# A four-layer image network on one core: halves of neighbouring images interleaved, GpSimd's adds moved to VectorE, and the offsets stage written out as a pipeline

## The chip, the core and the metric

The kernel runs on one core of a Trainium2 chip. The metric is the device time of one execution in microseconds. The engines go by the profile's names: PE (TensorE, with PEld for its weight loads), DVE (VectorE), ACT (ScalarE), POOL (GpSimd), and SP, which issues most of the DMAs. Each runs its own program; they meet at semaphores alone.

## The reference

x is (8, 32, 128, 128) float32: eight images of 32 channels. Four layers follow each other: a spectral convolution, a graph convolution with batch norm and residual, a layer of deformable line convolutions, and a closing 3x3 convolution. The third layer is the one that the change touches:

```python
out_standard = conv2d(x, conv_w, conv_b, padding=1)
offset_x = offset_branch(x, offx_...)   # depthwise 3x3, batch norm, relu, 1x1 to 9 channels
offset_y = offset_branch(x, offy_...)
out_x = dsc_axis(x, offset_x, dscx_w, 'x')
out_y = dsc_axis(x, offset_y, dscy_w, 'y')
out = conv2d(jnp.concatenate([out_standard, out_x, out_y], axis=1), fus_w, None, padding=0)
return relu(batchnorm(out, fus_bn_g, fus_bn_b))
```

`dsc_axis` samples the image at 9 taps per pixel, each moved along one axis by its own offset with linear interpolation and zeros outside, and sums taps and channels with a weight. The three branches are summed by the 1x1 fusion, so their results can be added in any order.

## The kernel before

The kernel is a row of stages with a barrier between them: `spectral_forward`, `spectral_mix`, `spectral_inverse`, `load_weights`, `graph_conv`, `residual_norm`, `depth_conv` (L897), `offsets` (L1002), `deformable` (L1427) and `closing`, with small batch-norm coefficient stages between. Results go through DRAM from stage to stage.

`depth_conv` makes, for chunks of 16 rows, the two depthwise branches (LX from X, LY from the transposed image XT) and the plain convolution (LP, from X), one group of six matmuls each (L975), ACT reads them out (L992) and issues the stores.

`offsets` turns the two branches into 18 offset maps and splits each into three bf16 parts (high, middle, low). Per image: SP loads both branches into one of two halves of HI (four DMAs of 1 MB, L1025), ACT rectifies them in four pieces (L1058), then for each of 8 chunks of 512 columns PE multiplies (L1077), ACT copies out of PSUM into t_o (L1063), GpSimd casts the high part (L1093), DVE subtracts it (L1109), GpSimd casts the middle part (L1096), DVE subtracts again (L1113), giving the low part. ACT waits for the low part of the chunk before (L1062, one chunk behind), and rectifies the next image only when all chunks of this one are out. SP stores an image's parts by four DMAs (L1031) and only then loads the image two further on. The loops are hardware loops over pairs of images.

`deformable` works on lines. An image has a y half (a=0, on the transposed image) and an x half (a=1), 32 steps of four image lines each (one per 32 partitions); such a step is called a line below, a half a phase. For each line, in three thirds: PE spreads the offsets of three taps against pixel positions (L1745), ACT and DVE take absolute values into T (L1614, L1659), GpSimd clips them to interpolation weights ("hats", L1576, one instruction a third, three a line), PE multiplies the image line by the tap weights (L1770, copied out by L1618 and L1664), and PE applies the hats, 72 matmuls a line (L1791). PE's program is two lines ahead with the spreads: after it applies a third of line n it spreads the same third of line n+2. T has two line buffers. DVE reads the line out of PSUM: in the y half into XO (L1670), which PE transposes (L1780), DVE gathers into YB (L1681), SP writes to DRAM (L1500) and loads back in the other layout into YR (L1505); in the x half (L1674) it adds to U, which SP had loaded with the plain result (L1497). GpSimd then adds YR to U, 64 adds in all, eight an image (`finish`, L1584), during the next image's y phase (in the last image, during its x phase and behind it), DVE takes batch statistics (L1695) and SP sends U out (L1492). Phases run in the order y0, x0, y1, x1, ... y7, x7. During a phase ACT normalises the next phase's image (L1631) and DVE sums its lines (L1686).

SP's order is written out by hand: each line it waits for the spreads (L1487), then issues what is listed for that line.

## Time and profile before

| | us |
|---|---|
| median of the runs shown | 4535.45 (4530.43 to 4545.91) |
| the profiled execution, its own time | 4534.85 |
| its span, first to last instruction | 4533.2 |
| mean granted TensorE clock | 0.898 |

The page gives each engine's busy time over the whole span. The span is made of stages with different limits, so it is read in stretches: the view of windows gives each engine's busy time, the granted clock (1.00 is 2.4 GHz, 0.50 is 1.2 GHz), the mean busy share of the 16 DMA engines and GB/s between two times. A timeline line gives start, duration, engine, line of the kernel, operation and tiles; in brackets the idle time before and what ended it. The ends of GpSimd's instructions are rough in this profile; the distance from start to start of instructions that follow each other is what can be trusted. The stages touched lie at 1109 to 1662 us (`depth_conv`), 1676 to 1939 us (`offsets`) and 1939 to 4251 us (`deformable`).

### The profile page before, as it was taken

The page shows a single profiled execution, that of the slowest core. Times are in us where ns is not written, and L with a number is a line of the kernel's source. Part 1 is how long each engine was busy: PE and PEld are TensorE (multiplying, and loading weights), DVE is VectorE, ACT ScalarE, POOL GpSimd, SP SyncE. Part 2 cuts the span into 40 slices and gives each one's busy share as a digit, 9 for nine tenths or more (in the row PEclk, how much of TensorE's full clock was granted, in tenths as well). Part 3 has the DMA queues.
Part 4 walks back from the last instruction along what each step waited for, and adds up shares of the span by engine and source line. Part 5 has one row for each costly group of instructions (what it writes and reads, how often), then busy time and mean ns, then how long its engine had stood idle before and what let it go on. Part 6 is the DMA issues. An engine that isn't in the chain of part 4 may idle for free. (4 is left out here: it accounts for less than half of the span.)

```text
span 4533.2 us, 143240 instructions
## 1 busy us (share of the span) xinstructions
PE 3639.5 (80%) x59682; PEld 2155.1 (48%) x59682; DVE 2529.5 (56%) x5104; ACT 2648.5 (58%) x2951; POOL 2475.7 (55%) x1851
## 2 busy tenths in 40 slices
PE   6866448533999965569999999999999999999488
PEld 5765445322333332236655555555555555555222
DVE  5302636543333324447776776767777667776455
ACT  5600004332222224469989889898898988988442
POOL 0000210011000003369999999999999999999600
PEclk9955659855999987779999999999999999999799
DMA  3265649998877865531112121122211212111585
GB/s 95 59 132 124 191 104 255 236 332 225 227 218 210 226 199 168 168 72 56 39 53 59 55 60 41 53 57 56 60 39 55 57 54 60 39 57 42 125 213 128
DMA packets 675524, 532.85 MB, mean 118 GB/s; under 512 B 39434, under 2 KB 600714, under 8 KB 667050
## 3 DMA queue, kind: packets, MB, share of 16 engines
q1 hardware_dynamic: 556444, 386.26, 33.4%
q10 hardware_dynamic: 108560, 105.02, 7.5%
q0 software_dynamic: 9984, 33.56, 2.3%
q8 instruction: 441, 7.23, 0.7%
q14 instruction: 95, 0.78, 0.1%
HBM read 338.51 MB, written 186.19 MB: 116 GB/s over the span
## 5 line engine op out<-in xcount | busy, mean ns | idle before, releaser
L1576 POOL TENSOR_SCALAR df_t<-df_t 128x1536 f32<-128x1536 f32 x1536 | 2225.2, 1806 | 51.2 <-ACT df_t L1614 51.0
L1791 PE MATMUL df_o<-df_t,df_zs 128*32 128x128 f32 x36864 | 1326.2, 277 | 121.1 <-POOL df_t L1576 87.9
L1659 DVE TENSOR_SCALAR df_t<-df_d 128x512 int32<-128x512 int32 x1536 | 1062.3, 692 | 551.8 <-PE df_d L1745 548.8
L1614 ACT ACTIVATE df_t<-df_a 128x1024 f32<-128x1024 f32 x1024 | 1051.4, 1027 | 241.7 <-PE df_a L1745 238.5
L1791 PEld LDWEIGHTS df_o<-df_t,df_zs 128*32 128x32 f32 x36864 | 916.1, 110 | 568.3 <-POOL df_t L1576 265.3
L1745 PE MATMUL df_d<-df_ix,net_sel 11*128 11x512 bf16 x1536 | 593.1, 386 | 1.0 <-DVE df_t L1659 0.9
L1614 ACT ACTIVATE df_t<-df_z 128x1024 f32<-128x1024 f32 x512 | 525.2, 1026 | 60.9 <-PE df_z L1745 24.7
L1618 ACT ACTIVATE df_zs<-df_z 128x864 f32<-128x864 f32 x512 | 453.2, 885 | 2.0 <-PE df_z L1770 2.0
L1745 PE MATMUL df_a<-df_ix,net_sel 11*128 11x512 bf16 x2048 | 398.8, 386 | 37.5 <-DMA df_ix<-offset 37.4
L1770 PE MATMUL df_z<-net_Z,df_x 32*128 32x288 f32 x4096 | 392.8, 427 | 17.9 <-ACT df_x L1631 9.9
L1093 POOL CAST of_parts<-of_t_o 128x512 bf16<-128x512 f32 x64 | 40.1, 626 | 646.4 <-ACT of_t_o L1063 646.4
L797 POOL DMA_DIRECT2D x_2t<-r_xt x32 | 28.2, 887 | 408.6 <-ACT r_xt L826 392.9
L1664 DVE COPY df_zs<-df_z 128x288 f32<-128x288 f32 x512 | 230.7, 450 | 26.2 <-PE df_z L1770 24.5
L975 PE MATMUL dc_c<-dc_x,net_LX 128*64 128x512 f32 x768 | 189.0, 624 | 55.3 <-DVE dc_xt L949 55.3
L461 ACT ACTIVATE iv_z<-iv_z 128x512 f32<-128x512 f32 x32 | 19.1, 597 | 346.9 <-PE iv_z L420 346.9
L1077 PE MATMUL of_f<-of_hi,net_PW 128*128 128x512 f32 x256 | 128.2, 665 | 109.3 <-ACT of_hi L1058 109.3
L1745 PEld LDWEIGHTS df_a<-df_ix,net_sel 11*128 11x128 bf16 x2048 | 96.4, 91 | 238.7 <-issue 173.7
L954 DVE BATCH_NORM_STATS2 net_sty<-dc_o 128x512 f32 x64 | 44.4, 694 | 284.5 <-ACT dc_o L992 284.5
L1745 PE MATMUL df_z<-df_ix,net_sel 11*128 11x512 bf16 x1024 | 199.4, 386 | 2.5 <-ACT df_zs L1618 0.6
L1313 PE MATMUL cl_c<-cl_xb,net_L 128*32 128x512 f32 x768 | 186.4, 642 | 14.7 <-ACT cl_xb L1183 14.7
L1770 PEld LDWEIGHTS df_z<-net_Z,df_x 32*128 32x128 f32 x4096 | 172.6, 184 | 53.4 <-ACT df_t L1614 25.4
L1313 PE MATMUL cl_c<-cl_xa,net_L 128*32 128x512 f32 x768 | 187.3, 645 | 3.4 <-DVE cl_xa L1253 3.4
(228 smaller groups left out, 4731.5 us busy)
## 6 DMA issues: line engine op xcount, KB each, us to landing
gc_x<-x SPq DMA_DIRECT2D x240, 128.0 KB, 4.8
dc_x<-x SPq DMA_DIRECT2D x240, 128.0 KB, 3.2
dc_xt<-x_2t SPq DMA_DIRECT2D x240, 128.0 KB, 4.6
fw_x<-in_x SPq DMA_DIRECT2D x32, 512.0 KB, 6.8
iv_x<-in_x SPq DMA_DIRECT2D x64, 256.0 KB, 4.7
x<-iv_x POOLq DMA_DIRECT2D x64, 256.0 KB, 4.9
y<-gc_o ACTq DMA_DIRECT2D x64, 256.0 KB, 5.8
r_y<-y SPq DMA_DIRECT2D x8, 2048.0 KB, 14.2
```

Source lines behind the costliest of these rows:

```text
L954: v.bn_stats(st[:, bass.ds(n, 1), :].rearrange("p a s -> p (a s)"), O[:, (j - 1) % 2, m]).then_inc(counted, 1)
L975: mm = pe.matmul(bank[64 * t:64 * t + 64, :], wt[w_][:, d, :], t_[:, k, t:R2:2, d:d + W], start=(d == 0), stop=(d == 2))
L1077: mm = pe.matmul(ps_f[c % 4][:], wt["PW"][:, m, :], HI[:, k, m, 512 * c:512 * c + 512], start=(m == 0), stop=(m == 1))
L1313: mm = pe.matmul(bank[r, :], wt["L4"][:, x, r], t[:, b % 2, k:k + 4, x:x + W], start=(x == 0), stop=(x == 2))
L1576: g.tensor_scalar(t, t, 1.0, 0.0, ALU.min, ALU.max).then_inc(hat_p, 1)
L1614: act.activation(T[:, m % 2, 3 * i:3 * i + 2], src, ACT.Abs).then_inc(a_read, 1)
L1618: act.activation(Zs[:, m % 2, 1:4, :], ps_z[:, 1:4, 0:32 * K9], ACT.Copy).then_inc(za_read, 1)
L1659: v.tensor_scalar(T[:, m % 2, 3 * i + 2].bitcast(I32), ps_d[:].bitcast(I32), 0x7fffffff, None, ALU.bitwise_and).then_inc(d_read, 1)
L1664: v.tensor_copy(Zs[:, m % 2, 0, :], ps_z[:, 0, 0:32 * K9]).then_inc(zd_read, 1)
L1745: return pe.matmul(out, wt["sel"][r, slot, :], ixv[r, :, P * j:P * j + P], start=True, stop=True)
L1770: mm = pe.matmul(ps_z[:, q, 0:32 * K9], X[a][r, P * j:P * j + P], wt["Z"][r, a, :], start=True, stop=True)
L1791: mm = pe.matmul(ps_o[32 * q:32 * q + 32, 0:P], Zs[:, m % 2, q, 32 * k:32 * k + 32], T[:, m % 2, 3 * i + x, P * q:P * q + P], start=(k == ...
```

## The change

Three edits go together.

In `depth_conv` the plain convolution is made from the transposed image (its weights are transposed too), so that the plain result lies as the y result does before it is turned.

In `offsets` the loops are written out; HI has three image buffers and t_o and t_r four chunk buffers; SP loads three images ahead and issues the load of image b+3, which waits for the last matmul of image b, ahead of the store of image b; ACT rectifies a quarter of the next image after every second chunk; GpSimd casts the high part of chunk n and then the middle part of chunk n-1, DVE subtracts for chunk n and then finishes chunk n-1. The parts have two image buffers as before.

In `deformable` the phases run y0, y1, x0, y2, x1, ... y7, x6, x7. The plain result is loaded into a tile UT of its own and added when DVE reads a y line; the turned y result is loaded back into U, where the x readout adds to it. `finish` and its 64 adds on GpSimd are gone, as is YR. Statistics and sends follow the x readout within the phase. The turned result of image 0 is gathered in the half of U that is not yet in use.

```diff
@@ depth_conv
-        kinds = ((X, "LX", "bx"), (X, "LP", "bp"), (XT, "LY", "by"))
+        kinds = ((X, "LX", "bx"), (XT, "LP", "bp"), (XT, "LY", "by"))
@@ offsets, SP
-                def store(b, k):
-                    sp.wait_ge(low, NCH * (b + 1) + 2)
...
-                with sp.Fori(1, B // 2) as i:
-                    for k in range(2):
-                        store(2 * i + k - 2, k)
-                        load(2 * i + k, k)
+                def load(b):
+                    if b >= NB:
+                        sp.wait_ge(full, NCH * (b - NB + 1))
+                    for e in range(2):
+                        for m, t in enumerate((hx, hy)):
+                            r = slice(N // 2 * e, N // 2 * (e + 1))
+                            sp.dma_start(HI[:, b % NB, m, r], t[b][:, r]).then_inc(h_in[b % NB], 16)
...
+                for b in range(NB):
+                    load(b)
+                for b in range(B):
+                    if b + NB < B:
+                        load(b + NB)
+                    store(b)
@@ offsets, ACT
+                for h in range(NH):
+                    rectify(0, h)
+                for n in range(NT):
+                    b, c = divmod(n, NCH)
+                    a.wait_ge(full, n + 1)
+                    if n >= ND:
+                        a.wait_ge(rest, n - ND + 1)
+                    a.activation(t_o[:, n % ND], ps_f[n % 4][:], ACT.Identity, bias=wt["pb"][:, 0:1]).then_inc(taken, 1)
+                    if c % 2 and b + 1 < B:
+                        rectify(b + 1, c // 2)
@@ offsets, GpSimd
+                for n in range(NT + 1):
+                    if n < NT:
+                        b, c = divmod(n, NCH)
+                        if c == 0 and b >= 2:
+                            g.wait_ge(sent[b % 2], 64 * (b // 2))
+                        g.wait_ge(taken, n + 1)
+                        g.tensor_copy(parts[:, b % 2, 0, pixels(n)], t_o[:, n % ND]).then_inc(high, 1)
+                    if n:
+                        g.wait_ge(rest, n)
+                        g.tensor_copy(parts[:, (n - 1) // NCH % 2, 1, pixels(n - 1)], t_r[:, (n - 1) % ND]).then_inc(mid, 1)
@@ offsets, DVE
+                for n in range(NT + 1):
+                    if n < NT:
+                        v.wait_ge(high, n + 1)
+                        if n >= ND:
+                            v.wait_ge(mid, n - ND + 1)
+                            v.wait_ge(low, n - ND + 1)
+                        v.tensor_tensor(t_r[:, n % ND], t_o[:, n % ND], parts[:, n // NCH % 2, 0, pixels(n)], ALU.subtract).then_inc(rest, 1)
+                    if n:
+                        v.wait_ge(mid, n)
+                        v.wait_ge(rest, n)
+                        v.tensor_tensor(parts[:, (n - 1) // NCH % 2, 2, pixels(n - 1)], t_r[:, (n - 1) % ND],
+                                        parts[:, (n - 1) // NCH % 2, 1, pixels(n - 1)], ALU.subtract).then_inc(low, 1)
@@ deformable
-        YB, YR = s.sb("yb", [P, C * W]), s.sb("yr", [P, LINES * W])
+        YB, UT = s.sb("yb", [P, C * W]), s.sb("ut", [P, LINES, W])
+        phases = [(0, 0)] + [(b + 1 - a, a) for b in range(B - 1) for a in range(2)] + [(B - 1, 1)]
@@ deformable, SP, line m of phase t
+                        if before[1] == 0:
+                            bt = before[0]
+                            if m == 1 and bt > 1:
+                                sp.wait_ge(u_out, 16 * NCH * (bt - 1))
+                                sp.wait_ge(counted, NCH * (bt - 1))
+                            if m == 5:
+                                sp.wait_ge(kept, LINES * (bt + 1))
+                            if 5 <= m < 13:
+                                put_turned(bt, m - 5)
+                            if m == 17:
+                                sp.wait_ge(uy_out, 128 * (bt + 1))
+                            if 17 <= m and m % 2 and (m - 17) // 2 < 8:
+                                get_turned(bt, (m - 17) // 2)
+                        c, r = divmod(m - 8, 4)
+                        if r == 0 and c >= 0:
+                            if a == 1:
+                                send(t, b, c)
+                            elif b + 1 < B:
+                                sp.wait_ge(o_read, LINES * t + SC * (c + 1) + 1)
+                                load_plain(b + 1, c)
...
+                    if a == 1:
+                        send(t, b, NCH - 1)
+                    elif b + 1 < B:
+                        sp.wait_ge(o_read, LINES * (t + 1) + 1)
+                        load_plain(b + 1, NCH - 1)
@@ deformable, GpSimd
-                def finish(b, par, c):
...
-                    g.tensor_tensor(ur, ur, YR[:, r], ALU.add).then_inc(summed, 1)
@@ deformable, DVE
-                        v.tensor_scalar(XO[:, m % 2], ps_o[:, 0:P], S[:, 0, j:j + 1], None, ALU.add).then_inc(o_read, 1)
+                        if j % (LINES // 2) == 0:
+                            v.wait_ge(ut_in[2 * j // LINES], 8 * NCH * (b + 1))
+                        v.scalar_tensor_tensor(out=XO[:, n % 2], in0=ps_o[:, 0:P], scalar=S[:, t % 2, j:j + 1], in1=UT[:, j],
+                                               op0=ALU.add, op1=ALU.add).then_inc(o_read, 1)
...
-                            v.wait_ge(u_in, 16 * NCH * (b + 1))
+                            v.wait_ge(u_in, 128 * (b + 1))
@@ weight_layouts
-        cw[:, p, :, p:p + 3] = c("conv_w").transpose(0, 3, 2, 1)
+        cw[:, p, :, p:p + 3] = c("conv_w").transpose(0, 2, 3, 1)
```

## Rows read from the trace of the kernel before

**Rows 1.** The page, part 1: busy time, share of the span and instructions.

```profile
PE 3639.5 (80%) x59682; PEld 2155.1 (48%) x59682; DVE 2529.5 (56%) x5104; ACT 2648.5 (58%) x2951; POOL 2475.7 (55%) x1851
```

**Rows 2.** Stretches: from:to, length, busy PE, PEld, DVE, ACT, POOL, clock, DMA share, GB/s.

```profile
1689.00:1938.70 249.70, 128.16 (x256) 54.47 (x256) 95.62 (x128) 107.79 (x96) 76.37 (x128) 0.75 0.56 173
...
1981.10:4247.50 2266.40, 2135.63 (x45742) 1292.16 (x45740) 1606.28 (x3002) 1994.69 (x2159) 2265.42 (x1593) 1.00 0.18 51
```

**Rows 3.** The same view by phases: y0, x0, y1, x1.

```profile
1981.10:2118.30 137.20, 136.39 (x2886) 84.63 (x2887) 103.17 (x202) 125.07 (x137) 136.22 (x97) 1.00 0.10 29
2118.30:2252.30 134.00, 133.13 (x2854) 81.16 (x2854) 95.98 (x169) 126.61 (x136) 134.00 (x95) 1.00 0.20 57
2252.30:2399.60 147.30, 137.21 (x2886) 82.88 (x2886) 107.98 (x210) 125.89 (x136) 147.30 (x105) 1.00 0.18 52
2399.60:2536.90 137.30, 130.70 (x2854) 78.79 (x2854) 94.48 (x170) 125.10 (x136) 137.30 (x97) 1.00 0.20 55
```

**Rows 4.** Timeline of GpSimd in phase y2: start us, us, engine line op, tiles, xcount.

```profile
2595.32 1.31 POOL L1584 TENSOR_TENSOR df_u<-df_u,df_yr 128x512 f32<-128x512 f32 x1
2596.56 12.94 POOL L1576 TENSOR_SCALAR df_t<-df_t 128x1536 f32<-128x1536 f32 x9
```

**Rows 5.** Timeline of the offsets stage, one chunk, idle time and releaser in brackets.

```profile
1764.10 0.61 POOL L1096 CAST of_parts<-of_t_r 128x512 bf16<-128x512 f32 x1 [1.31 <-DVE of_t_r L1109]
1764.66 0.61 POOL L1093 CAST of_parts<-of_t_o 128x512 bf16<-128x512 f32 x1
1764.89 0.92 DVE L1113 TENSOR_TENSOR of_parts<-of_t_r,of_parts 128x512 bf16<-128x512 f32 x1 [0.95 <-POOL of_parts L1096]
1765.74 0.68 DVE L1109 TENSOR_TENSOR of_t_r<-of_t_o,of_parts 128x512 f32<-128x512 f32 x1
1766.58 0.61 POOL L1096 CAST of_parts<-of_t_r 128x512 bf16<-128x512 f32 x1 [1.31 <-DVE of_t_r L1109]
```

**Rows 6.** Lines L1058 and L1077: duration ns min/median/max, first and last start.

```profile
L1058 ACT ACTIVATE of_hi<-of_hi,net_coy x16: 2077/2078/2083, 1691.0 to 1897.4; 128x2048 f32<-128x2048 f32 x16
L1077 PE MATMUL of_f<-of_hi,net_PW x256: 592/593/1193, 1693.5 to 1911.9; 128*128 128x512 f32 x128
```

**Rows 7.** Stretches of the offsets stage: loads alone, store alone, two of two pairs each.

```profile
1680.00:1696.00 16.00, 2.51 (x3) 1.17 (x4) 0.00 (x0) 6.98 (x4) 0.00 (x0) 0.50 1.01 426
1926.00:1934.00 8.00, 0.00 (x0) 0.00 (x0) 0.00 (x0) 0.00 (x0) 0.00 (x0) 0.50 0.52 121
1720.50:1773.90 53.40, 31.52 (x63) 13.21 (x61) 21.66 (x29) 20.90 (x22) 17.49 (x29) 0.76 0.72 223
1780.50:1832.30 51.80, 29.73 (x62) 12.42 (x61) 21.66 (x29) 20.23 (x21) 17.06 (x29) 0.82 0.73 227
```

**Rows 8.** Groups of instructions by line: shapes, count, busy us, mean ns, idle before.

```profile
L1674 DVE SCALAR_TENSOR_TENSOR df_u<-df_o,df_s,df_u 128x128 f32<-128x128 f32 x256 | 89.8, 351 | 80.3 <-PE df_o L1791 67.0
L1670 DVE TENSOR_SCALAR df_xo<-df_o,df_s 128x128 f32<-128x128 f32 x256 | 89.8, 351 | 29.6 <-PE df_o L1791 2.8
...
L1695 DVE BATCH_NORM_STATS2 net_stf<-df_u 128x6 f32<-128x512 f32 x64 | 43.8, 684 | 1.1 <-POOL df_u L1584 1.1
```

**Rows 9.** Timeline of DVE in phase y0, readouts of lines.

```profile
2023.22 0.35 DVE L1670 TENSOR_SCALAR df_xo<-df_o,df_s 128x128 f32<-128x128 f32 x1
2027.41 0.35 DVE L1670 TENSOR_SCALAR df_xo<-df_o,df_s 128x128 f32<-128x128 f32 x1
...
2058.98 0.35 DVE L1670 TENSOR_SCALAR df_xo<-df_o,df_s 128x128 f32<-128x128 f32 x1
```

**Rows 10.** Timeline of DVE at the end of the deformable stage.

```profile
4247.76 0.69 DVE L1695 BATCH_NORM_STATS2 net_stf<-df_u 128x6 f32<-128x512 f32 x1
...
4250.20 0.69 DVE L1695 BATCH_NORM_STATS2 net_stf<-df_u 128x6 f32<-128x512 f32 x1 [0.53 <-POOL df_u L1584]
```

**Rows 11.** Line L1505, loads of the turned y result: when they land.

```profile
DMA to landing us min/median/max: 3.0/3.4/8.7
```

**Rows 12.** Timeline of SP's DMA issues at the start of the deformable stage.

```profile
1961.20 10.43 SPq L1476 DMA_DIRECT2D df_x<-x  x16
```

More of the change, by code:

```diff
@@ L1565, in _ @@
-                images_in_turn(image)
+                    load_offsets(0, c)
                 for c in range(NCH):
-                    send(B - 1, (B - 1) % 2, c)
+                    load_plain(0, c)
+                for t in range(len(phases)):
+                    phase(t)
                 sp.wait_ge(u_out, 16 * NCH * B)
```

497 lines of the change are left out of this document (191 added, 306 removed).

## The prediction

> **What bounds the kernel now.** I read the page first: no engine is over 80% busy and the kernel is a row of stages, so the averages say nothing about a single edit [rows 1]. Then I cut the span at the stage borders, with the windows view [rows 2]. Two stages are touched by edits that can move time: the offsets stage (1676.5 to 1938.7 us) and the deformable stage (1939 to 4250 us). The depth convolution is touched as well, but only in which tile it reads.
>
> In the deformable stage the reader is to see GpSimd: 2265.4 of 2266.4 us busy between the first and the last line read out [rows 2]. Cut into phases of 32 lines, the x phases (a=1) take 137.3 us and the y phases (a=0) of images 1 to 7 take 147.3 us, both with GpSimd busy to the last tenth; the difference is eight GpSimd adds, L1584 [rows 3]. In the timeline nine hats, L1576, take 12.94 us, 1.43 to 1.44 each, and an add takes 1.24 until the next hat begins [rows 4]. 96 hats at 1.43 are 137.3 us: the phase is the sum of GpSimd's instructions. (The page's mean of 1806 ns for a hat is not used; the spacing is what adds up to the phase.)
>
> In the offsets stage no engine is full: over 249.7 us PE has 128, ACT 108, DVE 96, GpSimd 76 [rows 2]. Inside an image a chunk takes 2.48 us: GpSimd cast, DVE subtraction, GpSimd cast, DVE subtraction, with 0.16 us between the end of a subtraction and the next cast [rows 5]. Between images there are four rectifications of 2.08 us, two of them before the first matmul [rows 6]. Beside it runs the DMA. Loads alone move 426 GB/s at a share of 1.01 of the 16 engines; the store alone moves 121 GB/s at a share of 0.52; and while stores and loads of images alternate, two pairs (four times 6 MB in all, a store and a load each) take 53.4 and 51.8 us, 26.3 us a pair, with hardly a pause [rows 7]. That will be the second bound.
>
> **The change, part by part.**
>
> *Adds off GpSimd.* The 64 adds go. The plain result is now added where the y result leaves PSUM: L1670, a tensor_scalar of 351 ns, becomes the form of L1674, which costs 351 ns too [rows 8], so DVE pays nothing. The y result, which now carries the plain one, is loaded straight into U, and the x readout adds it as it added the plain result before. In seven phases the adds cost 147.3 - 137.3 = 10.0 us each, 70 us. In the last phase five lie before the last line read out, at 1.25 us 6.2 us. Three come behind it: the last bn_stats, which waits for the last add, begins at 4250.20 instead of 4247.76, right behind the last readout, and so does the last send [rows 10], 2.4 us. Sum 78.6 us.
>
> What is late next? PE. The first y phase, which has no adds, took 137.2 us with PE 136.4 busy, and the first x phase 134.0 us with PE 133.1 busy [rows 3]: these are PE's own rates, against GpSimd's 137.3. A y line takes PE 4.19 us (2023.22 to 2027.41 in phase y0), against 4.29 for three hats [rows 9]. So a y phase becomes a near tie. Lines during normalisation are slower, which GpSimd, up to two lines ahead in T, absorbs or not; I charge 0.35 us for each of eight y phases, 2.8 us. This leaves 75.8, say 76 us. If nothing hides PE, see the second rival.
>
> *Interleaved halves.* The order becomes y0, y1, x0, y2, x1 and so on, ending y7, x6, x7. The number of lines, matmuls, hats, transposes and copies is the same. The round trip of a y result through memory is issued in the phase behind it: the last piece is loaded once the spreads of that phase's 31st line are done, which is in PE's 29th line, and the x phase's first readout waits for it. It comes more than three lines, 3 x 4.29 = 12.9 us, later; the pieces land within 3.4 us, at most 8.7 us [rows 11]. Cost nothing. On SP the plain loads move into UT; SP now waits at the end of a phase for the last line read out, with the next phase's image loads queued behind it. They start some three lines later and are wanted from line 10 on; two a line at about 0.6 us each [rows 12]. Cost nothing. bn_stats (64 x 0.68 us, [rows 8]) move from y phases (DVE 108 us of 147.3) into x phases (94.5 of 137.3) [rows 3]; DVE has room there.
>
> *Start of the stage.* Eight plain loads take the place of sixteen loads of the second image behind the offset loads, from 1961.2 us on [rows 12]. The first readout at 1981.1 now waits for four of them; even at the 0.65 us of an image load each and 8.7 us to land they are there by 1973. Nothing.
>
> *Plain convolution from the turned image.* L975 reads XT in place of X for one of three groups, in the same shapes, and PE already waits for both tiles ahead of the first group. Nothing.
>
> *Offsets as a pipeline.* Three input buffers, four chunk buffers, GpSimd's second cast and DVE's second subtraction one chunk behind, and the next image's rectifications between chunks. I make the ledger by the DMA. Loads of three images at 426 GB/s (4.19 MB, 9.9 us each) run from 1678.9 to 1708.5. Rectification starts at 1689 as before and the first chunk leaves at about 1697.4. Then the ring holds L3 S0 L4 S1 L5 S2 L6 S3 L7 S4 S5 S6 S7, each pair costing the 26.3 us seen now. S3 ends at 1708.5 + 4 x 26.3 = 1813.7, S4 lands about 26 us later, at 1839.7. The parts buffers are two, so image 6 may be split only when S4 has landed, and image 7 behind image 6. With p for a chunk and 1.5 us for its tail, an image takes 8p + 1.5, and the end is 1839.7 + 2(8p + 1.5) + 1.1 for the issue + 14.9 for S7 (1.77 MB at 121 GB/s, with its start) + 1.5 to land.
>
> For p the trace shows no pipelined loop. From below it is DVE's two subtractions with nothing between, 0.68 + 0.92 = 1.6 us; from above the four operations one behind the other without any overlap, 0.61 + 0.61 + 0.68 + 0.69 = 2.6 us. I take 2.3, from the nearest row: in the loop of today GpSimd's cast and DVE's subtraction overlap only where L1113 grows from 0.69 to 0.92, and the four already fill 2.32 of 2.48 us [rows 5]. p = 2.3 gives an end at 1897 (42 us saved), 1.6 an end set by the DMA at about 1888 (51), 2.6 1902 (37). An image then takes 20 us, under the pair's 26.3, so p counts only behind the last load. PE has 128 us for 64 chunks, 2.0 a chunk at a mean clock of 0.75 [rows 2]; a matmul takes 592 ns at the full clock and up to 1193 at the lower one [rows 6], so PE fits under p, though each image may begin cold. That is 42 us.
>
> The Trainium skill speaks against this part: SBUF — State Buffer, "Who interferes with whom", says that a DVE instruction with two SBUF inputs and a GpSimd instruction that reads SBUF take one port pair in turn, the second blocked until the first is through. Both subtractions and both casts are of that kind. By that rule p is 2.6 and the pipeline gains nothing inside a chunk; the sum would be 113 instead of 118 us. The growth of L1113 to 0.92 agrees in kind, not in full: blocked for the cast's whole remainder it would be 1.07.
>
> **Sum.** 76 + 42 = 118 us off the profiled execution's 4534.85 us (its span is 4533.2): 4417 us. The median of the runs shown, 4535.45, is the same to 0.6 us.
>
> **Rivals.**
> 1. *One port in turn.* p = 2.6: 37 us in the offsets stage, 4422 us. For it: the 0.92; against: 2.48 already lies under 2.6. Chance 0.2.
> 2. *PE becomes the bound in the deformable stage.* In phase y0 the seven lines from 2027.41 to 2058.98, during normalisation, take 31.6 us, 1.5 over GpSimd's pace [rows 9]; unabsorbed in eight phases that is 12 us. The moved bn_stats, 0.68 us each, put some 10 us more on the chain if a fifth of the 44 us meets PE's wait for DVE. With 12 and 10 us less gain: 4439 us. Against it: GpSimd was full in x phases with the same normalisation. Chance 0.15.
> 3. *The offsets stage gives nothing*, because SP's queue holds stores behind loads and the mixed traffic slows further. 4459 us. Chance 0.08.
> 4. *More.* The seven engines that stores leave idle run ahead on loads and the pair falls to 22 us: five pairs, 20 us. 4397 us. Chance 0.07.
> 5. *Slower: the y result comes late.* The x phase's first readout waits for the memory round trip, all engines behind it. Half a phase's lead is gone, the 12.9 us above remain. In eight phases it must cost over 118 / 8 = 15 us each, so a piece must land 28 us after its issue, against 8.7 at most now. Just past that: 4552 us. Chance 0.03.
> 6. *The adds were cover for something else* (GpSimd's records being rough) and the phases stay at 147: only the offsets gain is left, 4493 us. Against it: x phases without adds run at 137.3 in the same trace. Chance 0.02.
>
> **How the numbers follow.** The forecast, 4417 us, has 0.45. From 4394 to 4450 takes in the bounds of p (4408 to 4422), rival 4, and rival 2 with half as much again, and leaves out rivals 3, 5 and 6, under 0.2. A measurement here tells about 0.3% (14 us) from no change. Faster by more than that: all but rival 5 and a rest of 0.01, 0.96; same 0.01; slower 0.03.
>
> **What would show it.** In the profile after: no L1584-like adds; all sixteen phases of 32 lines at 137 to 138 us with GpSimd full; PE within 1 us of that in y phases; last send right behind the last readout. In the offsets stage: the DMA without pause from the first load to the last store, an image every 26 us until the last load, then 20 us; the casts and subtractions at 2.3 us a chunk. The prediction fails if y phases are longer than 138, if stores and loads together move less than 225 GB/s, or if DVE waits for u or ut at a phase's start.

## The result and the profile after

The changed kernel takes 4389.64 us (median of 4 runs, 4387.39 to 4394.77) against 4532.94 (4525.93 to 4545.91) for the kernel before: a ratio of 0.9683, 95% interval 0.9669 to 0.9697. That is 143 us less, where 118 were forecast; the time lies 4.4 us below the low end of the range. The profiled execution took 4387.39 us with a span of 4385.3, 147.9 less than before, and all that follows is read from it.

First the page, part 1, against [rows 1]. PE, which does the same work, has 3644.4 us for 3639.5. GpSimd is 32 us down: 64 adds of 1.24 are gone (79 us), and 128 casts that took 0.61 each [rows 5] now take about 1.0 (in the offsets stage GpSimd has 122 us for 76, 46 up). DVE is 30 us up, by its stretched subtractions.

```profile
PE 3644.4 (83%) x59682; PEld 2156.9 (49%) x59682; DVE 2559.5 (58%) x5104; ACT 2639.7 (60%) x2951; POOL 2443.9 (56%) x1787
```

Then the windows view with the same columns as [rows 2]: the offsets stage from the first rectification, and the loop of the deformable stage from the first to the last line read out.

```profile
1685.00:1867.60 182.60, 122.82 (x256) 50.16 (x256) 126.40 (x128) 104.92 (x96) 122.48 (x128) 0.85 0.68 237
1910.10:4101.80 2191.70, 2137.58 (x45742) 1301.49 (x45739) 1606.37 (x3004) 1987.57 (x2158) 2189.47 (x1529) 1.00 0.18 53
```

By stages, each measured alike in both traces:

| stretch | before | after | less | forecast |
|---|---|---|---|---|
| all ahead of the offsets stage | 1676.2 | 1672.3 | 3.9 | 0 |
| offsets stage, to DVE's first work of the next | 263.3 | 195.6 | 67.7 | 42 |
| start of the deformable stage | 41.6 | 42.2 | -0.6 | 0 |
| its loop, first to last readout | 2266.4 | 2191.7 | 74.7 | 73.4 |
| last readout to the batch-norm aggregate's stage | 5.1 | 2.8 | 2.3 | 2.4 |
| closing | 270.7 | 270.8 | -0.1 | 0 |

(73.4 is 70 + 6.2 - 2.8 of the prediction. The aggregate's own stage, 9.9 us in both, is in no row.) The 3.9 us ahead of the offsets stage lie within what this part varies by: in the kernels below, none of which changes it any further, the stage begins anywhere from 1669.2 to 1685.8 us. So the deformable stage came out at 77 us for 76, and the miss is in the offsets stage.

*The deformable stage.* The same view by phases, to be read against [rows 3]: y0, y1, x0, y2, x1.

```profile
1910.10:2047.20 137.10, 136.32 (x2886) 84.60 (x2886) 103.14 (x202) 124.82 (x136) 135.86 (x95) 1.00 0.14 39
2047.20:2184.10 136.90, 136.10 (x2885) 84.39 (x2884) 103.08 (x201) 124.81 (x136) 136.90 (x97) 1.00 0.25 70
2184.10:2318.80 134.70, 133.43 (x2853) 81.01 (x2853) 99.86 (x176) 126.45 (x136) 134.70 (x95) 1.00 0.25 72
2318.80:2456.80 138.00, 136.63 (x2885) 83.59 (x2886) 103.67 (x202) 124.87 (x136) 138.00 (x98) 1.00 0.14 40
2456.80:2593.80 137.00, 131.80 (x2854) 79.44 (x2854) 98.67 (x177) 125.27 (x136) 137.00 (x96) 1.00 0.25 72
```

GpSimd is busy to the last tenth in y1, x0, y2 and x1 (in y0 it has 135.9 of 137.1, beside PE's 136.3), and the 147.3 us phases are gone: the six y phases from y2 on take 138.0 us each, the very limit that the prediction set, and the x phases behind x0 136.9 to 137.0 (x7, with a line less to its last readout, 133.3). Of the prediction's signs, "all sixteen phases at 137 to 138 us" fails for x0 alone, 134.7 us, as it was 134.0 before. The pair y2, x1 takes 275.0 us, where 192 hats at the 1.43 us of [rows 4] are 274.6. PE has 136.6 of 138.0 in y2. The turned y result's pieces land in 3.0 to 4.9 us, and in the groups below (shapes, count, busy, mean ns, idle before) no readout and no send waits for one: ahead of the x readout L1635 and the y readout L1630 only PE is named, and bn_stats, L1658, waits for nothing, where it waited for L1584 in [rows 8].

```profile
L1635 DVE SCALAR_TENSOR_TENSOR df_u<-df_o,df_s,df_u 128x128 f32<-128x128 f32 x256 | 89.8, 351 | 71.2 <-PE df_o L1744 55.1
L1630 DVE SCALAR_TENSOR_TENSOR df_xo<-df_o,df_s,df_ut 128x128 f32<-128x128 f32 x256 | 89.8, 351 | 28.0 <-PE df_o L1744 3.2
...
L1658 DVE BATCH_NORM_STATS2 net_stf<-df_u 128x6 f32<-128x512 f32 x64 | 43.7, 683 | 0.0
```

At the end bn_stats stands right behind the last readout, and nothing like the late 4250.20 of [rows 10] follows:

```profile
4101.80 0.35 DVE L1635 SCALAR_TENSOR_TENSOR df_u<-df_o,df_s,df_u 128x128 f32<-128x128 f32 x1 [3.94 <-PE df_o L1744]
4102.18 0.69 DVE L1658 BATCH_NORM_STATS2 net_stf<-df_u 128x6 f32<-128x512 f32 x1
```

*The offsets stage.* The windows view again: loads (at the start), three mixed stretches from the issue of one store to that of the next, and a store alone. To be read against [rows 7].

```profile
1676.00:1704.00 28.00, 14.87 (x28) 6.48 (x29) 6.49 (x8) 16.36 (x13) 6.34 (x9) 0.66 1.01 423
1735.80:1759.00 23.20, 15.98 (x33) 6.40 (x33) 15.87 (x17) 13.10 (x12) 15.38 (x17) 0.88 0.77 274
1759.00:1778.50 19.50, 16.42 (x33) 6.87 (x34) 15.92 (x17) 13.10 (x12) 15.43 (x17) 0.88 0.81 303
1778.50:1797.10 18.60, 14.88 (x33) 5.61 (x34) 15.84 (x17) 13.10 (x12) 15.35 (x17) 1.00 0.82 324
1853.00:1861.00 8.00, 0.00 (x0) 0.00 (x0) 0.00 (x0) 0.00 (x0) 0.00 (x0) 0.50 0.54 127
```

Loads alone and the store alone move what they moved before (423 for 426 GB/s, 127 for 121). But a pair takes 23.2, 19.5 and 18.6 us where 26.3 was the term of the sum, and moves 274 to 324 GB/s where [rows 7] have 223 and 227. The stages' own instructions show the second thing. First SP's issues, then GpSimd's (engine, line, tiles, idle time and releaser in brackets) around the start of an image:

```profile
1778.47 4.26 SPq L1038 DMA_DIRECT2D offset<-of_parts  x4
...
1797.11 60.08 SPq L1038 DMA_DIRECT2D offset<-of_parts  x16
```

```profile
1789.02 1.07 POOL L1089 CAST of_parts<-of_t_o 128x512 bf16<-128x512 f32 x1
1790.04 1.07 POOL L1092 CAST of_parts<-of_t_r 128x512 bf16<-128x512 f32 x1
1794.36 0.62 POOL L1089 CAST of_parts<-of_t_o 128x512 bf16<-128x512 f32 x1 [3.25 <-DMA offset<-of_parts]
1794.92 0.62 POOL L1092 CAST of_parts<-of_t_r 128x512 bf16<-128x512 f32 x1
```

```profile
1791.57 0.68 DVE L1106 TENSOR_TENSOR of_parts<-of_t_r,of_parts 128x512 bf16<-128x512 f32 x1
1795.01 1.07 DVE L1102 TENSOR_TENSOR of_t_r<-of_t_o,of_parts 128x512 f32<-128x512 f32 x1 [2.76 <-POOL of_parts L1089]
1796.00 1.09 DVE L1106 TENSOR_TENSOR of_parts<-of_t_r,of_parts 128x512 bf16<-128x512 f32 x1
```

In full flow casts follow each other by 1.02 us on GpSimd (1789.02 to 1790.04), and from one high cast to the next are 2.03 us, as on DVE from one first subtraction to the next: p is 2.03, all through the stage. At the border of two images it stops. The high cast of the next image's first chunk (1794.36) needs the parts buffer whose store went out at 1778.47, and waits 3.25 us for it. Behind it on GpSimd stands the middle cast of the *finished* image's last chunk (1794.92), behind that on DVE its last subtraction (1796.00), and behind that the store of the finished image (1797.11). So a store is never issued before the one ahead of it has landed, though there are two buffers. The view of line L1089 gives the sum of these waits:

```profile
L1089 POOL CAST of_parts<-of_t_o x64: 611/1067/1073, 1693.7 to 1845.8; 128x512 bf16<-128x512 f32 x64
...
  DMA offset<-of_parts: 28.8, 6
```

Neither the rate of the pairs nor this chain of stores was in the prediction.

### The profile page after: what moved, and what is told of

Same layout as the page of the kernel before. It is cut to its first block and busy times, and to the rows that moved or that the text cites. A ratio compares the mean times of both kernels' runs of the same rounds, so it can differ in the third digit from the quotient of the medians.

```text
span 4385.3 us, 142489 instructions
## 1 busy us (share of the span) xinstructions
PE 3644.4 (83%) x59682; PEld 2156.9 (49%) x59682; DVE 2559.5 (58%) x5104; ACT 2639.7 (60%) x2951; POOL 2443.9 (56%) x1787
## 5 line engine op out<-in xcount | busy, mean ns | idle before, releaser
L1563 POOL TENSOR_SCALAR df_t<-df_t 128x1536 f32<-128x1536 f32 x1536 | 2200.0, 1570 | 51.3 <-ACT df_t L1573 51.2
L1573 ACT ACTIVATE df_t<-df_z 128x1024 f32<-128x1024 f32 x512 | 525.8, 1027 | 36.3 <-PE df_z L1700 5.4
L1089 POOL CAST of_parts<-of_t_o 128x512 bf16<-128x512 f32 x64 | 64.0, 1000 | 615.6 <-ACT of_t_o L1066 586.8
L1621 DVE COPY df_zs<-df_z 128x288 f32<-128x288 f32 x512 | 230.9, 451 | 26.6 <-PE df_z L1724 26.2
L975 PE MATMUL dc_c<-dc_x,net_LX 128*64 128x512 f32 x768 | 189.6, 626 | 55.3 <-DVE dc_xt L949 55.3
L886 PE MATMUL r_t<-net_eye,r_x 128*128 128x128 f32 x256 | 57.9, 419 | 146.9 <-DVE r_x L851 75.5
```

The costliest lines, as they stand in the source:

```text
L886: mm = pe.transpose(ps_t[m % 4][:, P * r:P * r + P], X[:, k, (4 * m + r) * P:(4 * m + r + 1) * P], turn[1])
L975: mm = pe.matmul(bank[64 * t:64 * t + 64, :], wt[w_][:, d, :], t_[:, k, t:R2:2, d:d + W], start=(d == 0), stop=(d == 2))
L1089: g.tensor_copy(parts[:, b % 2, 0, pixels(n)], t_o[:, n % ND]).then_inc(high, 1)
L1563: g.tensor_scalar(t, t, 1.0, 0.0, ALU.min, ALU.max).then_inc(hat_p, 1)
L1573: act.activation(T[:, n % 2, 3 * i:3 * i + 2], src, ACT.Abs).then_inc(a_read, 1)
L1621: v.tensor_copy(Zs[:, n % 2, 0, :], ps_z[:, 0, 0:32 * K9]).then_inc(zd_read, 1)
```

## The experiments

Two theories were to be told apart. Mine, formed on this trace: the offsets stage before was bound by its own loop of casts and subtractions, its DMA merely kept pace, so the 26.3 us were never a price of the DMA; what sets the new stage is the DMA and, on top, the chain of stores at the border. (The second half of it stood; "merely kept pace" did not, see the old stage below.) The rival: the DMA was the bound, as the prediction had it, and the change made the DMA itself faster.

### Each part by itself

e1_offsets_only is the kernel before with only the offsets stage of the change (its buffers, semaphores and the programs of all five engines, from L1007 on); e2_deform_only is the changed kernel with the old offsets stage in its place.

> The kernel before with the new offsets stage alone; the deformable stage and the plain convolution as before. If the two edits are independent, the gain is what the offsets stage shows in the trace after, 67 us: about 4466 us, ratio 0.985. If part of the gain of the offsets stage came only together with the other edit, or if the ledger of the prediction (42 us) was right for this edit alone, about 4491 us, ratio 0.991.

> The changed kernel with the old offsets stage: interleaved halves, no GpSimd adds, plain convolution from the turned image. Theory: the deformable loop is GpSimd's hats alone, 192 x 1.43 = 274.6 us for a pair of phases; gain 77 us, about 4456 us, ratio 0.983. Rival, the edits hide each other's cost: the gain is the rest of 143 less what the offsets stage alone gives.

e1 took 4474.46 us, ratio 0.9883 (0.9865 to 0.9901); e2 took 4463.32, ratio 0.9847 (0.9826 to 0.9867). The offsets stage of e1 and the loop of e2:

```profile
1671.60:1873.80 202.20, 124.68 (x256) 51.62 (x256) 126.31 (x128) 104.86 (x96) 122.35 (x128) 0.81 0.69 236
```

```profile
1685.80:1947.70 261.90, 128.34 (x256) 54.38 (x256) 96.10 (x129) 107.83 (x96) 75.99 (x128) 0.74 0.58 182
1990.50:4183.10 2192.60, 2138.72 (x45742) 1302.11 (x45739) 1606.71 (x3004) 1987.64 (x2158) 2189.15 (x1529) 1.00 0.18 53
```

e1's stage is 202.2 us and e2's 261.9; e2's loop is 2192.6, 73.8 less than before. So each part does its own work, and neither leans on the other for the bulk of it. e1's ratio lies between the two expected, 0.985 and 0.991, but its stage decides: 61 us less, not 42. By the ratios the two gains add up to 122 us, against 143 for both. Most of the rest can be placed. e1's offsets stage is 6.6 us longer than that of the whole change, all of it in GpSimd's waits for stores (35.6 us in 6, against 28.8), its casts come every 2.03 us just the same; why its stores are slower is open. And e2's offsets stage happened to begin at 1685.8 us, 13.5 later than in the whole change, in a part that is the same in both.

### The DMA without the computing, and the computing without the DMA

e4_dma_alone is the changed kernel with all chunk work of images 2 to 7 cut to 32 of 512 columns (a rectification to 128 of 2048), and with the last middle cast and subtraction of an image ahead of the wait. e5_compute_alone keeps the work and cuts the transfers to a sixteenth, the loads from image 3 on and the stores from image 1 on.

```diff
+        def cols(n):
+            return 512 if n < 2 * NCH else 32
...
-            return slice(512 * (n % NCH), 512 * (n % NCH) + 512)
+            return slice(512 * (n % NCH), 512 * (n % NCH) + cols(n))
```

and in e5:

```diff
-                            r = slice(N // 2 * e, N // 2 * (e + 1))
+                            r = slice(N // 2 * e, N // 2 * e + (N // 2 if b < NB else 128))
...
+                        w_ = N if b == 0 else 256
+                        sp.dma_start(off[b][:, :, q, 0:w_], parts[32 * q:32 * q + 2 * K9, b % 2, :, 0:w_]).then_inc(sent[b % 2], 16)
```

> The changed kernel with the work of a chunk in the offsets stage cut from 512 to 32 columns from image 2 on (the offset maps are left mostly unwritten in value, all loads and stores are as large as before), and at an image's first chunk the chunk before is finished first. It shows the DMA's own pace. The prediction's term: a load and store pair 26.3 us, so the stage takes 190 us or more. Rival: the 26.3 us were set by the compute loop (8 x 2.45 us and the rectifications), and the pair costs 20 us or less by DMA alone; the stage then takes 165 us or less, the stretch with loads and stores together moves 300 GB/s.

> The changed kernel with the offsets stage's loads cut to a sixteenth from image 3 on and its stores to a sixteenth from image 1 on (the later stage reads image 0's offsets for every image). It shows the pace of the compute loop without DMA waits. If GpSimd's casts and DVE's subtractions take one port in turn, each blocked for the other's whole length: 2.6 us a chunk, 21 us an image. If they merely slow each other as the trace after shows in its densest stretch (an operation every 1.01 us on each engine): 2.03 us a chunk, 16.3 us an image, stage about 155 us. If PE bounds it at the full clock: 1.8 us a chunk.

e4's stage takes 169.4 us, between the 190 and the 165 expected and close to the rival: the whole of it, then three pairs, then the time in which only the last load's rest and stores are left.

```profile
1675.20:1844.60 169.40, 70.07 (x256) 52.37 (x256) 46.40 (x130) 46.84 (x96) 45.61 (x128) 0.59 0.75 282
1737.60:1759.70 22.10, 7.22 (x34) 7.01 (x34) 2.68 (x16) 3.33 (x12) 2.74 (x16) 0.50 0.88 331
1759.70:1778.00 18.30, 7.49 (x36) 7.28 (x35) 2.60 (x16) 3.33 (x12) 2.77 (x16) 0.50 0.81 319
1778.00:1796.30 18.30, 6.92 (x32) 6.71 (x33) 2.68 (x16) 3.32 (x12) 2.73 (x16) 0.50 0.70 287
1785.00:1803.00 18.00, 7.19 (x32) 6.98 (x32) 2.68 (x16) 3.44 (x13) 2.73 (x16) 0.50 0.57 238
```

A load and a store of an image cost the DMA 18.3 us, 22.1 for the first. The last row shows how. Its share of 0.57 is nine of sixteen engines (0.56), and its 238 GB/s are 9/16 of the 426 that loads move alone, about twice what a store alone moves (127, at 0.54). ACT waits for the last load until 1802.9, and from 1784 on 10.7 MB move, where the five stores not yet landed have at most 8.9. So from 1784 on, where the share falls, seven engines are through with their part of the last load, and the nine that also carry the stores still move it. The share of all sixteen is under 1 here although hardly anything is computed: in this stage it can't be read as pauses. e5's stage takes 162.3 us (155 were expected, with the same 2.03 us a chunk), and once its loads are small both engines are full:

```profile
1669.20:1831.50 162.30, 117.04 (x256) 47.37 (x256) 128.23 (x128) 104.47 (x96) 126.76 (x128) 0.89 0.29 102
1746.20:1795.00 48.80, 44.12 (x97) 17.20 (x96) 48.80 (x50) 39.03 (x37) 48.80 (x49) 1.00 0.07 18
```

So the new stage of 195.6 us has two bounds of nearly the same height, 169.4 by the DMA and 162.3 by GpSimd and DVE (p = 2.03 there too, with hardly any DMA traffic: it is not the DMA that stretches the casts), and 26 us more than the higher of them.

### The old stage without its computing

This is the run that decides between the theories. e10_before_dma_alone is the kernel *before*, its loads, stores, queue order and buffers untouched, with the chunk work cut to 32 columns (and the buffers cleared once).

```diff
-                            px = slice(512 * c, 512 * c + 512)
+                            px = slice(512 * c, 512 * c + 32)
...
-                            g.tensor_copy(parts[:, k, 0, px], t_o[:, c % 2]).then_inc(high, 1)
+                            g.tensor_copy(parts[:, k, 0, px], t_o[:, c % 2, 0:32]).then_inc(high, 1)
```

> The kernel before, with the work of a chunk in the offsets stage cut to 32 columns (the offset maps are mostly not computed; all loads and stores are as large as before). It tests the reading on which the prediction's ledger rested. If a load and store pair costs the DMA 26.3 us, as read, the images follow at 26 us still and the stage takes about 240 us. If the 26.3 us were the compute loop's own period, the images follow at 20 us or less and the stage takes about 185 us.

Its stage takes 196.4 us for 263.3, with the same bytes in the same order. The whole, and three stretches from the issue of one store to that of the next:

```profile
1677.00:1873.40 196.40, 56.42 (x256) 55.37 (x256) 24.57 (x128) 31.44 (x96) 46.81 (x129) 0.50 0.70 243
1748.70:1773.00 24.30, 7.01 (x32) 6.90 (x32) 3.07 (x16) 3.94 (x12) 3.27 (x16) 0.50 0.75 269
1773.00:1794.00 21.00, 7.01 (x32) 6.90 (x32) 3.07 (x16) 3.94 (x12) 3.28 (x16) 0.50 0.80 286
1794.00:1815.20 21.20, 7.01 (x32) 6.90 (x32) 3.07 (x16) 3.94 (x12) 3.27 (x16) 0.50 0.78 308
```

The pairs are 21.0 and 21.2 us, 24.3 for the first of them, not 26.3 (20 or less were expected for a stage of 185). The old DMA could do more than it was asked for, and the rival falls in the main. A part of it stays: with the computing cut in both, a pair takes 21.0 us here and 18.3 in e4. Whether the third buffer, the loads issued ahead of the stores or the border makes these 2.7 us was not tried.

But the DMA did not merely keep pace either. In the trace of before, the last subtractions of images 0 to 3 end at 1718.5, 1744.1, 1778.0 and 1803.4, so 25.6, 33.9 and 25.4 us apart. 25.5 us is the computing of an image: eight chunks of 2.48 us and the rectifications between them. The rest is a wait of ACT for loads, ahead of images 2, 4 and 6: their load stands behind a store in SP's queue, and that store waits for the computing. Line L1058 has these waits in one sum, 36.3 us in four, 13.6 of them for the very first load, and the timeline has the one ahead of image 2.

```profile
  DMA of_hi<-branch_y: 36.3, 4
```

```profile
1747.76 2.09 ACT L1058 ACTIVATE of_hi<-of_hi,net_cox 128x2048 f32<-128x2048 f32 x1 [7.57 <-DMA of_hi<-branch_y]
```

The stretches of [rows 7] take in two pairs each and leave out the pause behind them. The first of them, cut where S1 is issued, and the pause, in the kernel before:

```profile
1718.70:1744.40 25.70, 16.35 (x32) 6.96 (x32) 12.09 (x16) 9.29 (x10) 9.46 (x16) 0.77 0.73 216
1744.40:1773.00 28.60, 16.76 (x32) 7.09 (x32) 8.72 (x12) 12.86 (x11) 8.03 (x13) 0.74 0.71 224
1773.00:1779.00 6.00, 0.61 (x1) 0.50 (x2) 3.08 (x5) 5.65 (x4) 1.78 (x3) 0.50 0.00 0
```

The first pair lasts until the computing lets S1 go. The second waits for no computing: it is a store and a load by themselves (but for the first 3 us, in which the load before still ends), the load issued 7.3 us behind the store, with no next pair to fill its end. So 26.3 was the mean of a time set by the computing and of a pair that stood alone, and neither is the price of a pair where the next stands ready behind it.

### The border between images

The chain of stores should hold a part of these 26 us. e3_border takes it away: at an image's first chunk GpSimd and DVE first finish the chunk before.

```diff
                 for n in range(NT + 1):
+                    border = n % NCH == 0
+                    if n and border:
+                        cast_mid(n - 1)
                     if n < NT:
...
-                        g.wait_ge(taken, n + 1)
-                        g.tensor_copy(parts[:, b % 2, 0, pixels(n)], t_o[:, n % ND]).then_inc(high, 1)
-                    if n:
-                        g.wait_ge(rest, n)
-                        g.tensor_copy(parts[:, (n - 1) // NCH % 2, 1, pixels(n - 1)], t_r[:, (n - 1) % ND]).then_inc(mid, 1)
+                        cast_high(n)
+                    if n and not border:
+                        cast_mid(n - 1)
```

cast_high(n) and cast_mid(n) are the two casts with their waits; VectorE's two subtractions are ordered in the same way.

> The changed kernel; at an image's first chunk GpSimd and DVE finish the chunk before first, and only then GpSimd waits for the parts buffer. Theory: in the changed kernel the last middle cast of image b stands behind the wait for the store of image b-1 on GpSimd, so stores never overlap, and the stages's images follow at store time plus 2.8 us, 18.3 to 20 us. With the order turned, two stores can be in flight, the images without loads beside them follow at 15.5 to 16.3 us; the offsets stage ends 5 to 8 us sooner, about 4383 us. Rival: DMA alone sets 18.3 us a pair and the wait only hid inside it: 2 us or less.

The stage falls to 188.6 us, 7.0 less. GpSimd's order at the border is now the middle cast first, and the wait behind it:

```profile
1795.72 1.07 POOL L1092 CAST of_parts<-of_t_r 128x512 bf16<-128x512 f32 x1
...
1801.36 1.17 POOL L1088 CAST of_parts<-of_t_o 128x512 bf16<-128x512 f32 x2 [2.95 <-DMA offset<-of_parts]
```

The waits for stores are 18.0 us in 6, for 28.8. The kernel took 4382.99 us, ratio 0.9673 (0.9648 to 0.9698): the 7 us stand in the profile, while the interval of the whole kernel overlaps that of the change. e11_border_halves goes on from there and sends each image in two halves, the first as soon as four chunks are ready:

```diff
-                def store(b):
-                    sp.wait_ge(low, NCH * (b + 1))
+                def store(b, e):
+                    sp.wait_ge(low, NCH * b + NCH // 2 * (e + 1))
+                    r = slice(N // 2 * e, N // 2 * (e + 1))
...
+                    store(b, 0)
                     if b + NB < B:
                         load(b + NB)
-                    store(b)
+                    store(b, 1)
```

> The changed kernel with the turned order at the image border and the stores in two halves, but both subtractions reading SBUF as in the changed kernel. It tells which edit carries the gain of the kernel with all three (0.9634). Theory, the stage is bound by the DMA: a chunk at 1.85 to 2.03 us in place of 1.47 costs only behind the last load, 2 to 4 us: about 0.964. Rival, the faster chunk carries it: 0.967, as with the order alone.

Its stage takes 179.3 us and the kernel 4374.79, ratio 0.9638 (0.9619 to 0.9657). e12_changed_again, the changed kernel once more beside it, took 4386.61, ratio 0.967 (0.9652 to 0.9688), with a stage of 195.5: the stage's length repeats to 0.1 us. The runs of e11 (4368.99 to 4375.3) and of e12 (4385.52 to 4389.1), on one chip, lie apart.

> The changed kernel itself once more, on the same chip as the next two. Two traces of the same new offsets stage differ so far: 195.6 us in the changed kernel, 202.2 us where it stood alone. If a stage that the DMA bounds varies by that much from execution to execution, it comes out between 190 and 205 us here, and the time at 0.968 to 0.970 of the kernel before. If the two edits help each other, it is 195 to 196 us again.

### The first subtraction out of PSUM

What stretches the casts from 0.61 to 1.07 us and the subtractions from 0.68 to 1.09? e7_border_psum is e3 with one more edit: the first subtraction reads the convolution's result in PSUM (eight PSUM buffers for four) and adds the bias itself, so that it has only one SBUF input.

```diff
-                    v.tensor_tensor(t_r[:, n % ND], t_o[:, n % ND], parts[:, n // NCH % 2, 0, pixels(n)], ALU.subtract).then_inc(rest, 1)
+                    v.scalar_tensor_tensor(out=t_r[:, n % ND], in0=ps_f[n % 8][:], scalar=wt["pb"][:, 0:1],
+                                           in1=parts[:, n // NCH % 2, 0, pixels(n)], op0=ALU.add, op1=ALU.subtract).then_inc(rest, 1)
```

> The kernel before this one, and DVE's first subtraction reads the chunk from PSUM (with the bias added in the same instruction) in place of t_o, with eight PSUM banks. It then has one SBUF input. Theory, port in turn for two SBUF inputs against a GpSimd read: this subtraction no longer slows beside a cast (0.7 us in place of 1.09), the other still does, a chunk takes 1.6 us in place of 2.03, and the time falls by another 0 to 4 us, because DMA is by then the bound. Rival, any DVE instruction slows GpSimd alike: 2.03 us stays.

GpSimd and DVE in full flow, in this kernel:

```profile
1834.47 0.61 POOL L1089 CAST of_parts<-of_t_o 128x512 bf16<-128x512 f32 x1
1835.03 1.06 POOL L1093 CAST of_parts<-of_t_r 128x512 bf16<-128x512 f32 x1
1836.04 0.61 POOL L1089 CAST of_parts<-of_t_o 128x512 bf16<-128x512 f32 x1
```

```profile
1833.97 0.74 DVE L1111 SCALAR_TENSOR_TENSOR of_t_r<-of_f,net_pb,of_parts 128x512 f32<-128x512 f32 x1
1834.64 0.98 DVE L1117 TENSOR_TENSOR of_parts<-of_t_r,of_parts 128x512 bf16<-128x512 f32 x1
```

A chunk takes 1.57 us for 2.03. The first subtraction is no longer stretched (0.74 us in its new form). The high cast begins beside it and is back at 0.61, though most of it, from 1834.64 to 1835.08, runs beside the subtraction with two SBUF inputs; that one began later, and it is the one stretched, to 0.98, as is the middle cast, 1.06, that begins beside it. The stage takes 182.9 us, 5.7 less than e3's. The kernel took 4383.15, ratio 0.9669 (0.9645 to 0.9693), the same as e3 within the runs: the 5.7 us are shown by one profile, not by the times. e9_all has all three edits.

> The kernel before this one, with the stores of an image in two halves, the first issued after four chunks. The last store, exposed for 17.3 us at the end of the stage, becomes half as long: 8 us less, about 4372 us. Rival: rows of 4 KB in place of 8 KB cost the DMA engines more each byte, and the stage, bound by DMA, gives it back: 4380 us or more.

It took 4365.6 us (4362.97 to 4370.11), ratio 0.9634 (0.9617 to 0.965), an interval clear of the changed kernel's, and 21 to 24 us under its two medians: it beats both kernels. e11, without the PSUM edit, has 0.9638, the same as far as times can tell (its stage is 8.1 us longer): the border and the halves carry the gain that the times show.

```profile
1677.70:1848.90 171.20, 118.23 (x256) 50.99 (x256) 97.25 (x130) 102.76 (x96) 96.53 (x128) 0.85 0.74 279
```

Its stage, 171.2 us, is 24.4 under the changed kernel's: 7.0 from the border (e3), 5.7 from PSUM (e7), 11.7 from the halves. That it ends 2 us over the 169.4 of e4 does not show that only the DMA is left. e4 sends its stores whole, and in e9 the DMA still stands nearly still once, behind the last load:

```profile
1815.50:1819.50 4.00, 4.00 (x11) 1.77 (x10) 4.00 (x7) 4.00 (x6) 4.00 (x6) 1.00 0.06 26
```

### The hats made shorter

e8_small_hats is the changed kernel with hats on two of three taps, to see how far PE lies under GpSimd.

```diff
-                        t = T[:, n % 2, 3 * i:3 * i + 3].rearrange("p k n -> p (k n)")
+                        t = T[:, n % 2, 3 * i:3 * i + 2].rearrange("p k n -> p (k n)")
```

> The changed kernel with each hat instruction of GpSimd in the deformable stage on two of its three taps (the third tap's weights are left unclipped). It shows the next bound under GpSimd. Theory: PE is next and close: y phases 136.5 to 137 us, x phases 134 us, the loop 17 to 20 us shorter than in the changed kernel's trace. Rival: there is more room under GpSimd, and the phases fall to 125 us or less.

```profile
2322.60:2459.70 137.10, 136.30 (x2886) 84.48 (x2886) 103.69 (x203) 125.07 (x137) 99.52 (x98) 1.00 0.15 40
2459.70:2594.20 134.50, 133.47 (x2853) 81.11 (x2850) 100.03 (x176) 126.55 (x136) 99.18 (x96) 1.00 0.25 73
1912.60:4078.10 2165.50, 2151.16 (x45742) 1321.89 (x45739) 1617.92 (x3004) 2000.62 (x2158) 1582.97 (x1529) 1.00 0.19 53
```

With GpSimd at 99 us a phase, y phases take 137.1 us and x phases 134.5, and the loop 2165.5 for 2191.7, 26.2 less where 17 to 20 were expected: PE, with what it waits for of DVE and ACT, lies 0.9 us under GpSimd in a y phase and 2.5 in an x phase.

## Why the prediction was right and where it was wrong

*Adds off GpSimd, 78.6 us less 2.8 for PE.* Right, in size and in its parts. The loop is 74.7 us shorter for 73.4 and the tail 2.3 for 2.4. The middle y phases take 138.0 and the x phases 137.0, against 137.3 at GpSimd's own rate before; a pair is 0.4 us over 192 hats, where the prediction charged 0.35 for its y phase. e8 shows the near tie it spoke of, 0.9 us. Rival 2, PE as the bound for 22 us more, falls by the same run, and rival 6 by the phases. The point that looked most at risk, GpSimd's records being rough, did not matter, since the phase had been read from spacings.

*Interleaved halves at no cost.* Right: no wait for the turned y result, pieces there within 4.9 us for 8.7. Rival 5 did not come about; how late the result would have to be was not tried.

*Start of the stage, plain convolution, moved bn_stats.* Within 0.6 us of nothing.

*The ledger of the DMA, 42 us.* Wrong, by 25.7 us, and by one term of the sum: "each pair costing the 26.3 us seen now". Laid beside the trace, with the stage beginning 4.2 us earlier than forecast:

| step | forecast | less 4.2 | measured | off |
|---|---|---|---|---|
| S3 has landed | 1813.7 | 1809.5 | 1794.3 | 15.2 |
| S4 has landed | 1839.7 | 1835.5 | 1812.6 | 7.7 more |
| from there to the end | 57.3 | 57.3 | 55.3 | 2.0 more |

Up to S4 it is the price of the pairs, 22.9 of 24.9 us. The reading that failed stands in the prediction's own words, "with hardly a pause". The pauses lay between the two stretches of [rows 7]: the DMA moves nothing from 1773.0 to 1779.0, and the stores of the old stage go out 25.4 and 33.5 us apart in turn (means), not 26.3. Inside a stretch, one pair lasted as long as the computing of an image, 25.7 us, and the other, 28.6 us, was a pair by itself; without the computing the same transfers take 21 us (e10), and in the changed kernel a pair takes 18.6 to 23.2. The 26.3 was made credible by a coincidence: a load alone and a store alone, one behind the other, are 9.9 + 14.9 = 24.8 us. What hides a part of this sum is that a store uses nine engines, and the other seven run ahead on the loads meanwhile.

*A wait that was missed.* The prediction named the two parts buffers, but only for images 6 and 7, and not what is queued behind the wait for them: the last middle cast, the last subtraction and the store. Against a stage without that order it costs 7.0 us (e3). That error had the other sign: with the pairs priced right and this missed, the forecast would have come out too low.

*p.* 2.3 was taken between 1.6 and 2.6; it is 2.03 (e5, and all stretches of the changed kernel), so 4.3 us less for the last sixteen chunks. They were given back: image 7 could start only when S5 had landed, and GpSimd waited 4.55 us for it at 1832.5. That "p counts only behind the last load" held in the main: with p down by 0.46 us the stage lost 5.7 us in e7, where sixteen chunks make 7.4 and sixty-four 29.

*Rivals 1, 3 and 4.* Rival 1, one port in turn with p = 2.6, falls by the 2.03; its price falls, its mechanism does not (next paragraph). Rival 3, mixed traffic that slows further, falls by 274 to 324 GB/s. Rival 4 had the direction: 22 us a pair and 4397. Its chance of 0.07 was too small, and so was its step: the pair came to 18.6 to 23.2. Its mechanism, idle engines that run ahead on loads, is in e4's last row: 238 GB/s at a share of 0.57.

*The rule of the Trainium skill.* SBUF — State Buffer, "Who interferes with whom", has a DVE instruction with two SBUF inputs and a GpSimd instruction that reads SBUF take the port pair in turn, one blocked until the other is through. The stretching to 1.07 and 1.09 us, and the subtraction that reads PSUM in e7, 0.74 us beside a cast as anywhere, agree with the rule's condition. The size does not, if each instruction is charged with the whole time it takes alone: in turn the four would need 2.59 us a chunk, and 2.03 was measured. But the rows fit turns over a part of each instruction. In [rows 5] the stretched subtraction ends 0.54 us after the cast beside it (1765.27 to 1765.81), and in e7 too (1835.08 to 1835.62), with the middle cast ending 0.47 after that. In the full flow of the changed kernel the ends alternate between the engines, 1790.09, 1790.62, 1791.11, which are 0.53 and 0.49 us: together the 1.02 of a cast and a subtraction. Turns of about half a microsecond are an estimate from these ends, and GpSimd's ends are rough; no run here tells them from two instructions that only slow each other. What failed is the price of 2.6; that the rule itself failed is not shown.

*The range.* It reached to 4394 because the ledger's bounds were taken for p alone. The term that carried most of the 220 us, the pair, was given no bounds at all, though one stood in [rows 7]: with the pauses squeezed out, 53.4 x 0.72 / 2 = 19.2 and 51.8 x 0.73 / 2 = 18.9 us a pair, if the share of sixteen engines is taken for pauses. That is a low bound and no price, since a store alone leaves the share at 0.52. Five pairs at 19 for 26.3 are 36 us, and a low end at 4381 would have held the time.

## What to carry to other kernels

Where transfers run beside a computing loop, the period seen is no price of the DMA. Look at the time between the stretches that are measured as well as inside them, and ask for each issue whether it waited for computing; then take the computing away and look. A mean share under 1 decides nothing by itself: it was 0.72 in the old stage's stretches, and 0.75 in e4 with most of the computing gone, because the stores use nine of sixteen engines. Where two steps of a pipeline are skewed by one chunk, look at each wait for a buffer for what of the chunk *before* is queued behind it; finish that first, then wait. The widest range belongs to the term that carries the sum, not to the one that is argued about.

## What the runs showed of the hardware

- A load and a store of an image cost less together than one behind the other. Alone they take 9.9 us (4.19 MB at 426 GB/s) and 15.1 us (the changed kernel's last two stores, 3.54 MB from 1836.2 to 1866.5), 25 in all; in a stream of both 18.3 in e4 and 21.0 in e10. The store alone moves 121 to 127 GB/s at a share of 0.52 to 0.54, so about half of the engines' time is free beside it. That fits the Trainium skill, DMA: Bandwidth & Descriptors, "How many engines (k)" under "Why a DMA increments its semaphore by 16 and not by 1": the number of engines, at most 16, divides the slowest dimension, and 18 partitions give 9 of 16. The trace agrees, 9/16 being 0.56.
- A DMA share of 0.57 of sixteen engines went with 238 GB/s while load data was moved (e4) and one of 0.54 with 127 GB/s for a store alone: per engine a load moves twice as fast as a store.
- The same cast took 0.61 or 1.07 us and the same subtraction 0.68 or 1.09, by what ran beside it. In the changed kernel's full flow each cast and each subtraction was long, and with hardly any DMA traffic as well (e5); in e7 the cast that had begun before the subtraction with two SBUF inputs stayed at 0.61.
- One and the same offsets stage took 195.6 and 195.5 us in the changed kernel, and 202.2 in e1, by longer waits for its stores. The cause is open.
